# A feed-forward layer with routed experts: the block tokens in a ring of their own, two accumulators from block 33 on, and ScalarE's queue at the end

## The reference, cut to what matters

```
x1     = x_c + o @ wo                         # after attention; x_c is the first feed-forward's output
h      = rms(x1, ff_ln_w)
topv, topi = top_k(h @ wg, 4)                 # 16 experts, 4 for each token
gate   = softmax(topv)
a      = silu(h @ w1[e]) * (h @ w3[e])        # for each expert e
moe    = sum over the 4 experts: gate_e * (a @ w2[e])
out    = x + (x1 + moe)
```

## Time and profile before

| what | value |
|---|---|
| median of 3 runs | 519.99 us (519.49 to 520.69) |
| profiled execution, its own time | 519.2 us |
| span of that execution, first to last instruction | 517.4 us |
| mean granted TensorE clock | 0.997 of full speed |
| PE busy | 486.7 us (94%) |
| PEld busy | 411.8 us (80%) |
| DVE busy | 356.2 us (69%) |
| POOL busy | 270.7 us (52%) |
| ACT busy | 215.9 us (42%) |

### The profile page before, as it was taken

One profiled execution on the slowest core, in us unless ns is written; L12 is line 12 of the kernel. 1 busy time (PEld: TensorE's weight loads), 2 busy tenths in 40 slices (PEclk: granted clock), 3 DMA queues, 4 the chain that ended last, 5 costly groups with the idle time before them and its releaser, 6 DMA issues.

```text
span 517.4 us, 9264 instructions
## 1 busy us (share of the span) xinstructions
PE 486.7 (94%) x2965; PEld 411.8 (80%) x2965; DVE 356.2 (69%) x694; ACT 215.9 (42%) x476; POOL 270.7 (52%) x279
## 2 busy tenths in 40 slices
PE   7899999998989999999999999888799998999877
PEld 3788888887776898989798989776378887878765
DVE  3534241235888989999989898986488666666575
ACT  1322223224333333343343433434177566777660
POOL 2686611104686626252565556655235576777660
PEclk9999999999999999999999999999999999999998
DMA  8988789999642020101030312977786556666578
GB/s 281 306 271 275 249 255 340 339 340 341 190 142 64 1 52 2 42 0 42 3 86 0 92 37 64 341 260 262 254 259 101 99 98 102 97 103 99 94 145 254
DMA packets 67137, 82.53 MB, mean 159 GB/s; under 512 B 20993, under 2 KB 57090, under 8 KB 67074
## 3 DMA queue, kind: packets, MB, share of 16 engines
q1 hardware_dynamic: 56338, 61.16, 39.4%
q0 software_dynamic: 10752, 20.78, 17.9%
HBM read 45.54 MB, written 33.24 MB: 152 GB/s over the span
## 4 chain that ended last, share of the span: by engine, by line
PE 54%; DVE 15%; DMA 14%; issue 7%; POOL 4%; ACT 3%; SPq 1%; POOLq 0%; ACTq 0%; DVEq 0%
PE ringA L1464 19%; PE wide L1464 14%; PE ringT L1464 11%; DMA moe_acc<-y,xs 6%; DMA xs<-moe_rows 4%; DVE z L1137 4%; PE ringT L1572 3%; PE wide L1882 3%; DVE oT_lo L1117 2%; POOL moe_acc L728 2%; DMA staging<-in_cond_w 1%; DVE qs L1055 1%; DVE qc L1055 1%; DMA head_hi<-in_cond_head 1%; PE wide L1849 1%
## 5 line engine op out<-in xcount | busy, mean ns | idle before, releaser
L728 POOL DMA_INDIRECT moe_acc<-y,xs x45 | 82.5, 1832 | 55.4 <-ACT y L739 42.1
L592 POOL TENSOR_TENSOR qr<-qc,qs 128x256 f32<-128x256 f32 x80 | 56.9, 736 | 34.7 <-DVE qs L1055 33.5
L1464 PE MATMUL ringT<-ew,xsT_hi 128*128 (+1 forms) x188 | 60.3, 402 | 0.5 <-DVE xsT_lo L1336 0.5
L1464 PE MATMUL ringA<-qkvw_hi,hT_hi 128*128 128x512 f32 x96 | 40.7, 424 | 4.2 <-DVE qs L1055 3.5
L635 POOL DMA_INDIRECT moe_rows<-hx,slot x32 | 32.8, 1026 | 15.1 <-issue 8.1
L1464 PE MATMUL ringA<-qkvw_hi,hT_lo 128*128 128x512 f32 x96 | 37.7, 392 | 0.0
L1464 PE MATMUL ringA<-qkvw_lo,hT_hi 128*128 128x512 f32 x96 | 37.6, 391 | 0.0
L1464 PE MATMUL ringT<-ew,xsT_lo 128*128 (+1 forms) x94 | 37.0, 394 | 0.0
L1464 PEld LDWEIGHTS ringT<-ew,xsT_hi 128*128 128x128 f32 x188 | 32.0, 189 | 4.9 <-DVE xsT_lo L1336 0.8
L1351 DVE TENSOR_TENSOR w_lo<-ew,w_hi 128x512 fp32r<-128x512 f32 x31 | 21.5, 692 | 20.0 <-ACT w_hi L738 20.0
L1464 PE MATMUL ringA<-wo_hi,oT_hi 128*128 128x256 f32 x112 | 34.8, 310 | 0.0
(11 more groups left out here) (303 smaller groups left out, 1515.5 us busy)
## 6 DMA issues: line engine op xcount, KB each, us to landing
moe_rows<-fill SPq DMA_DIRECT2D x8, 2208.0 KB, 19.7
ew_raw<-in_expert_w SPq DMA_DIRECT2D x16, 512.0 KB, 5.9
xs<-moe_rows SPq DMA_DIRECT2D x47, 138.0 KB, 2.6
staging<-in_cond_w SPq DMA_DIRECT2D x8, 576.0 KB, 4.1
cw_hi<-in_cond_w POOLq DMA_DIRECT2D x8, 576.0 KB, 5.5
v_blk<-v SPq DMA_DIRECT2D x32, 128.0 KB, 3.4
ew<-in_expert_w SPq DMA_DIRECT2D x16, 256.0 KB, 6.4
qkvw_hi<-in_qkv_w POOLq DMA_DIRECT2D x6, 512.0 KB, 5.6
```

The source lines that it names most:

```text
L592: last = pool.tensor_tensor(rot[:, :, f, :], cos[:, :, f, :], sin[:, :, 1 - f, :], ALU.add)
L728: pool.indirect_dma_start(out=acc_dram[ACC[b]], out_offset=bass.IndirectOffsetOnAxis(xs[:, b % XSR, TOKEN:TOKEN + 1].bitcast(I32), 0), in_ ...
L1464: mm = pe.matmul(out, a, b, start=first and i == 0, stop=last and i == 2, skip_group_check=True)
```

## The change

The token numbers get a ring of 16 columns of their own, `tok`: DVE copies each block's 128 numbers there behind the split of its rows (45 copies in all), and the scatter reads them from `tok`. `rows_in(b)` now waits until ACT has scaled block b - 8 (`y_done`), not until that block's scatter has landed. LATE becomes 47 - 8 - 6 = 33: accumulators 0 and 1 take turns for blocks 33 to 44 and not only for 39 to 44, and the third accumulator is last used by block 32. SP's four loads of it now wait for scatters 32, 34, 36 and 38. At the end SP keeps the four loads of accumulator 0 and the first and third of the four stores; ACT's queue, behind all other work of ACT, issues the four loads of accumulator 1 and the second and fourth store.

```diff
--- before.py
+++ after.py
@@ -68,7 +68,8 @@
 PLACED = 2
 LAST = NBLK - 1
 SENT = NBLK - PLACED
-LATE = NBLK - XSR
+LATE = NBLK - XSR - 2 * NACC
+TOKR = 16
 ACC = [b % NACC if b < LATE else (b - LATE) % 2 for b in range(SENT)]
 NTH = [ACC[:b + 1].count(ACC[b]) for b in range(SENT)]
 assert SENT % YR + 1 < YR and LATE % NACC == 0
@@ -233,6 +234,7 @@
         blk_exp = sb("blk_exp", [1, NDYN], I32)
         col_i = sb("col_i", [P, P], I32)
         col_f = sb("col_f", [P, P])
+        tok = sb("tok", [P, TOKR], I32)
         last_tok = sb("last_tok", [P, PLACED])
         tile_tok = sb("tile_tok", [P, PLACED, NT])
         y_parts = nc.alloc_sbuf_tensor_at("y_parts", [P, 2, D], F32R, offset=y_at + 4 * D * (SENT % YR))
@@ -484,8 +486,7 @@
             def rows_in(b):
 
                 if b >= XSR:
-                    old = b - XSR
-                    sp.wait_ge(y_out[ACC[old]], 16 * NTH[old])
+                    sp.wait_ge(y_done, b - XSR + 1)
                 if b < NE:
                     src = rows_dram[ORDER[b] * T:ORDER[b] * T + P, :]
                 else:
@@ -508,20 +509,20 @@
             sp.wait_ge(y_out[2], 16 * ACC.count(2))
             sp.wait_ge(x1_out, 16 * 2)
             for h in range(NT // 2):
-                b = LATE + h - 1
+                b = LATE - 1 + 2 * h
                 sp.wait_ge(y_out[ACC[b]], 16 * NTH[b])
                 tiles = slice(2 * h, 2 * h + 2)
                 sp.dma_start(resid[:, tiles, :], acc_tiles[2][:, tiles, :]).then_inc(third_in, 16)
             sp.wait_ge(m_full, NBLK)
-            for i, b in enumerate((SENT - 2, SENT - 1)):
-                a = ACC[b]
-                sp.wait_ge(y_out[a], 16 * NTH[b])
-                for h in range(NT // 2):
-                    tiles = slice(2 * h, 2 * h + 2)
-                    sp.dma_start(acc_rows[a][:, tiles, :], acc_tiles[a][:, tiles, :]).then_inc(acc_in[i * NT // 2 + h], 16)
+            b = SENT - 2
+            sp.wait_ge(y_out[ACC[b]], 16 * NTH[b])
             for h in range(NT // 2):
+                tiles = slice(2 * h, 2 * h + 2)
+                sp.dma_start(acc_rows[ACC[b]][:, tiles, :], acc_tiles[ACC[b]][:, tiles, :]).then_inc(acc_in[h], 16)
+            last_rows_out = acc_rows[ACC[SENT - 1]]
+            for h in range(0, NT // 2, 2):
                 sp.wait_ge(out_rows, h + 1)
-                sp.dma_start(out_dram[:, 2 * h:2 * h + 2, :], acc_rows[a][:, 2 * h:2 * h + 2, :]).then_inc(out_done, 16)
+                sp.dma_start(out_dram[:, 2 * h:2 * h + 2, :], last_rows_out[:, 2 * h:2 * h + 2, :]).then_inc(out_done, 16)
             sp.wait_ge(out_done, 16 * (NT // 2))
 
 
@@ -726,7 +727,7 @@
                     pool.iota(col_i[:, :], pattern=[[1, P]], base=0, channel_multiplier=0).then_inc(cols_set, 1)
                 wait(pool, y_out[ACC[b]], 16 * (NTH[b] - 1))
                 pool.indirect_dma_start(out=acc_dram[ACC[b]],
-                                        out_offset=bass.IndirectOffsetOnAxis(xs[:, b % XSR, TOKEN:TOKEN + 1].bitcast(I32), 0),
+                                        out_offset=bass.IndirectOffsetOnAxis(tok[:, b % TOKR:b % TOKR + 1], 0),
                                         in_=y[:, b % YR, :], in_offset=None, bounds_check=T + P - 1, compute_op=ALU.add
                                         ).then_inc(y_out[ACC[b]], 16)
 
@@ -969,6 +970,16 @@
                     expert_hi(b + 3)
                 if b < NBLK:
                     silu(b)
+
+            a = ACC[SENT - 1]
+            last_acc = acc_dram[a][0:T, :].rearrange("(t p) d -> p t d", p=P)
+            act_e.wait_ge(y_out[a], 16 * NTH[SENT - 1])
+            for h in range(NT // 2):
+                tiles = slice(2 * h, 2 * h + 2)
+                act_e.dma_start(acc_rows[a][:, tiles, :], last_acc[:, tiles, :]).then_inc(acc_in[NT // 2 + h], 16)
+            for h in range(1, NT // 2, 2):
+                act_e.wait_ge(out_rows, h + 1)
+                act_e.dma_start(out_dram[:, 2 * h:2 * h + 2, :], acc_rows[a][:, 2 * h:2 * h + 2, :]).then_inc(out_done, 16)
 
 
         @block.vector
@@ -1334,6 +1345,8 @@
             def rows_lo(b):
                 dve.wait_ge(xsT_hi_done, b + 1)
                 dve.tensor_tensor(**lo_part(xsT_lo[:, b % 2, :], xs_bank[b % 2], xsT_hi[:, b % 2, :])).then_inc(xsT_lo_done, 1)
+                if b < SENT:
+                    dve.tensor_copy(tok[:, b % TOKR:b % TOKR + 1], xs[:, b % XSR, TOKEN:TOKEN + 1].bitcast(I32))
 
             def act_turned(b):
                 if b < NE:
```

## The result

| | kernel before | changed kernel |
|---|---|---|
| median | 523.52 us (519.49 to 527.85, 20 runs) | 517.43 us (515.41 to 521.19, 20 runs) |
| ratio, 95% interval | | 0.9905 [0.9881, 0.9928] |
| profiled execution, its own time and span | 519.2, 517.4 us | 520.99, 519.3 us |
| the same, kernels run again on another chip | 518.29 us (23 runs) | 513.83 us (6 runs), ratio 0.9909 [0.9873, 0.9945] |

The account below looks back on a forecast made before the run. Bound: the loop of scatter, landing, row load and scaling, 11.91 us per four blocks against TensorE's 10.16. Terms -7.2 + 0 + 1.9 - 0.3 = -5.6, taken as -5.4: 519.99 becomes 514.6 us, forecast 512.9 to 516.4, wider 511.8 to 517.9.

Parts of the forecast that it names:

- Part 1: Dynamic expert blocks: row loads released by `y_done` end TensorE's waits for `xs`, -7.2 us (at least 4.7, at most 8.7).
- Part 2: DVE's 45 copies of token numbers: hidden in DVE's idle time, 0 us (bounds 0 and 6.6).
- Part 3: Two accumulators, blocks 33 to 44: `resid` burst lengthens scatter 38's landing, scatter 44 starts 2.3 us late, +1.9 (-0.3 to +6.5).
- The bounds that I gave by part 3 alone: Range stated for the terms' bounds by the two-accumulator wait alone: -7.5 to -0.2 us.
- Part 4: End of the kernel on SP's and ACT's queues: saves only an issue gap, -0.3 us (-1.8 to +0.5).
- the rival: End of the kernel: two queues carry more, so SP alone is 1.5 us or more slower; no chance given.
- (a): Scatters of blocks 33 to 44 keep up despite the burst of three loads: 512.1 us, chance 0.17.
- (b): Scatters become the clock of the last twelve blocks, landings 5.0 us throughout: 517.8 us, chance 0.12.
- (c): Slower than before by the two-accumulator wait, landings of 5.9 us or more; 522.6 us at 6.4, chance 0.05.
- (d): Row loads come no sooner because another slot or table holds SP: about 519.5 us, chance 0.04.

Follow-up runs that it names:

- e1: Kernel before plus only the ring `tok` and row loads released by `y_done`; accumulators and end as before: ratio 0.9913 to the kernel before.
- e6: Kernel before plus the ring `tok` and its 45 copies, row loads still waiting for the scatter's landing: ratio 1.0021 to the kernel before.
- e8: Changed kernel without the four loads of the third accumulator and the waits for them, its share missing from the result: ratio 0.9896 to the kernel before.
- e5: The changed kernel again, no edit, on another chip: ratio 0.9909 to the kernel before, median 513.83 us.
- e3: Changed kernel with the end put back on SP's queue alone: ratio 0.9923 to the kernel before.
- e7: Changed kernel with the four `resid` loads spread, one behind each row load of blocks 43 to 46: ratio 0.9905 to the kernel before, median 513.95 us.
- e10: Changed kernel with the `resid` loads late, one each after scatters 38 to 41: ratio 0.9915 to the kernel before.
- e12: Changed kernel with LATE back at 39 and `resid` loads after scatters 38 to 41, same kernel as e4: ratio 0.9931 to the kernel before.
- e9: Kernel before with only the end on two queues (ACT's loads and stores), no ring, LATE 39: ratio 0.9995 to the kernel before.
- e4: Changed kernel with LATE back at 39 and `resid` loads after scatters 38 to 41: ratio 0.9922 to the kernel before.
- e2: Kernel before with only two accumulators from block 33 and `resid` loads after scatters 32, 34, 36, 38: ratio 1.0018 to the kernel before.
- e11: Changed kernel with each of the four third-accumulator loads issued twice, second to a spare array: ratio 0.9962 to the kernel before, median 515.88 us.

## Why the prediction was right or wrong

**The change itself was forecast at its size.** -5.4 us of 519.99 is -1.04%; measured were -0.95% [-1.19, -0.72] and -0.91%, and the medians of the first series differ by 6.1 us. The absolute time of 514.6 was not met: it was 517.43, above the forecast's 516.4 though inside the wider range to 517.9; by the ratio 0.9905 of the longer series' 523.52 it would be 518.5. The step that failed is the last of the sum, "it stood 0.8 below the median 519.99, which becomes 514.6". I took three runs within 1.2 us of each other for the kernel's level. Twenty runs of the same kernel, these three among them, had 519.49 to 527.85 and a median of 523.52, 3.5 us higher; my three are among the four lowest. With 523.52 for 519.99 the same sum gives 518.1. In the experiments the same kernel's medians were 518.33, 518.29 and 517.68. The changed kernel's 20 runs go from 515.4 to 521.2 with the granted clock: the seven with a clock of 0.997 or more have 515.41 to 517.02, the four of 0.986 to 0.989 have 519.56 to 521.19. The profile shows one such execution, which came to the first block 5.9 us later than the kernel before. A range for a time must hold this scatter, and mine was made of the change's terms alone. Why such executions were more frequent in the first series isn't settled.

**Part 1** (-7.2): right in mechanism. 70.69 became 63.51 in the changed kernel, and all kernels with the earlier release have this 63.51; e1 has it alone. No wait of TensorE for `xs` is left. Ring y held no one. The size was read off one execution: by the four profiles with the old wait the release is worth 5.1 to 7.2 us, and 7.2 is the most of them.

**Part 2** (0): right. e6 is 1.0021 [0.9989, 1.0052], and with the copies in place the blocks come at the full pace of TensorE. The Trainium skill's rule on the shared port of VectorE and GpSimd ("SBUF — State Buffer", "Who interferes with whom") would have added 0.15 us to each link; scatters in e8 keep step with their scalings to 0.0 in many blocks with a copy in each, and in e6 a copy ran during 29 of the 45 scatter instructions, which took 1.54 to 2.02 us as in the kernel before, block for block mostly within 0.01 us. No run here shows such a cost.

**Part 3** (+1.9): right in the lengthened landing and its handing on, not in what the long stretch adds. The lag of scatter 44 rose by 2.4 in the first profile, and by 1.3 in e5. Scatter 38 landed in 6.2 in e5, 2.0 above the median, where I took 2.2; scatter 39, expected at 5.5 or more, landed in 4.4. e8 confirms that the wait itself is nearly free. What I didn't foresee is that the same chain at LATE = 39 has nearly the same lag (0.7 to 1.6), so the part is neither a gain nor a loss that can be told. One premise was wrong: that landings away from the loads are 4.2 to 4.3. The kernel before already had some of 4.5 to 4.7 there, and e8, without any such load, has 5.2 for scatter 32; e1, e3, e7, e10 and e12 have 5.0 to 5.3 for the same scatter, though their first 256 KB load comes at block 35 or later, and e1 has 5.3 for scatter 23. I had named landings over 5 us away from the loads as a sign of being wrong. They were single ones with three accumulators in turn, and no lag grew from them; what lengthened them stays open. The bounds that I gave by part 3 alone, -7.5 to -0.2, don't follow from its terms either: they are -7.8 and -1.0.

**Part 4** (-0.3): not to be told from 0: e9 0.9995, e3 within the interval. Nor do these intervals exclude the 1.5 us of the rival. The rule that several issuing engines share the 16 DMA engines (the Trainium skill, "DMA: Bandwidth & Descriptors", "Issuing engines are not separate DMA queues") fits e9's 0.9995, which is too wide in its interval to prove it.

**What the sum lacked.** In the first profile the blocks gave -7.2 and the lag +2.4, and from scatter 44's start to the end were 15.2 us and not 14.5, +0.7; together that is the -4.1 of the stretch. The +0.7 is a landing of scatter 44 in about 4.9 and not 3.8 us, +1.1, less 0.4 behind it. The sum had no term for this landing. In e5, with the lag at 1.7 and the clock kept, the stretch is 85.3, -6.2 against before: -7.2 + 1.3 and, with 14.2 us from scatter 44's start to the end, -0.3.

**The rivals.** (a), keeping up, was nearly true of e8 alone, which has no third loads. (b) and (c) would have needed landings of 5 to 6 us throughout; e7 is what comes nearest, with four of 4.6 to 5.7, and there the lag stayed at 3.0 or less. (d) is refuted by e1 and e6 together.

## What to carry to other kernels

Look for the smallest thing that holds a ring's slot: here 128 token numbers kept 138 KB waiting for a transfer's landing, and copying them out had no cost that could be seen, and the earlier release took away 5 to 7 us of stalls. A chain of transfers that must wait for each other's landing, with only 0.1 us to spare per pair of blocks, hands most of a disturbance on to its end, so count the bulk loads that run beside it: doubling them cost 2 us, while spreading the four brought nothing. And forecast a ratio; an absolute time from three runs is worth no more than the spread between series and executions.

## What the runs showed of the hardware that was not expected

An accumulating scatter of 128 rows of 1 KB mostly landed 3.6 to 4.4 us after its start, but single ones took up to 5.3 with no load of 256 KB near (scatter 32 in e8: 5.2; scatter 23 in e1: 5.3). Beside one such load it took 3.8 to 5.7 (e4, e7, e10, e12), beside three 6.2 and 6.3 (e5, e3), beside four 6.6 (e2), and beside six 6.5 and 8.2 (e11). At the end it mattered when the loads came: begun 0.6 to 0.7 us after the scatter's start they went with a landing of 4.9 to 5.2, begun 1.7 us or more after it with 3.7 to 4.1, over fourteen profiles; one of 4.9 at 1.4 us doesn't fit. Four loads spread over four scatters were no better than three in a burst and one later. In one execution an unexplained wait of 2.2 us of VectorE ahead of the blocks was followed by a granted clock of 0.62 to 0.70, and it came to the first block 5.9 us late.
